# A Mamba and expert-choice kernel: stage 1's steps at other slots of the chunk, the expert stage written out without a loop

## What is computed

```python
x, z  = split(h @ in_proj_w.T)                  # 512 + 512 channels
u     = silu(causal_conv4(x) + conv_b)
dt, B, C = split(u @ x_proj_w.T, [16, 16, 16])
delta = softplus(dt @ dt_proj_w.T + dt_b)
state = exp(delta * A[n]) * state + delta * B[n] * u     # 16 states n, along the 2048 tokens
y     = sum_n C[n] * state + u * D
x1    = layernorm(x_in + (y * silu(z)) @ out_proj_w.T)
scores = softmax(x1 @ gate_w.T)                 # 8 experts
# each expert takes its 2048 highest tokens:
out   = gelu(layernorm(x1[idx]) * ln_w + ln_b @ fc1 + b1) @ fc2 + b2
x2    = x1; x2[idx] += out * score
return layernorm(x1 + x2)
```

## Time and profile before

| | |
|---|---|
| median of 3 runs | 4649.29 us (4644.24 to 4654.29) |
| the profiled execution | 4637.58 us, its span 4635.8 us |
| stage 1, first scan to last | 67.6 to 3470.5 us |
| stage 2 | 3530 to 3642 us |
| stage 3 | 3642 to about 4530 us, matmuls from 3706.7 to 4520 us |
| busy over the span | DVE 84%, PE 80%, POOL 76%, ACT 75% |
| granted TensorE clock, mean | 0.886 of full |

### The profile page before, as it was taken

The page is one execution under the profiler, slowest core; times in us unless marked ns, Lnnn a source line. Parts: engine busy times, 40 slices in busy tenths (PEclk is TensorE's granted clock), DMA queues, the critical chain, the costliest instruction groups (busy, mean ns, idle before and its releaser), DMA issues. The chain is left out here.

```text
span 4635.8 us, 58286 instructions
## 1 busy us (share of the span) xinstructions
PE 3700.9 (80%) x19154; PEld 2583.8 (56%) x19154; DVE 3909.9 (84%) x4971; ACT 3474.8 (75%) x5860; POOL 3515.7 (76%) x1714
## 2 busy tenths in 40 slices
PE   7788888888888888888888888888853199999990
PEld 3455555555555555555555555555542188888880
DVE  4899999999999999999999999999994677767645
ACT  5888888888888888888888888888860056555555
POOL 3888888898888888888888888888871156666643
PEclk9899899998988889989999998899965599999995
DMA  2666666665666666656665666666652123333328
GB/s 75 137 141 150 152 154 155 146 155 137 146 146 149 147 153 148 154 143 154 146 153 138 149 158 145 150 149 153 143 123 39 51 53 60 73 61 61 62 33 294
DMA packets 179913, 594.87 MB, mean 128 GB/s; under 512 B 33424, under 2 KB 99088, under 8 KB 128160
## 3 DMA queue, kind: packets, MB, share of 16 engines
q0 software_dynamic: 70368, 335.06, 36.8%
q1 hardware_dynamic: 104640, 239.32, 16.8%
q10 hardware_dynamic: 4608, 16.78, 0.9%
HBM read 221.47 MB, written 68.68 MB: 63 GB/s over the span
## 5 line engine op out<-in xcount | busy, mean ns | idle before, releaser
L433 POOL TENSOR_TENSOR dbu<-du,bb 128x2048 f32<-128x2048 f32 x512 | 2376.0, 4688 | 257.3 <-DVE h L793 229.4
L793 DVE TENSOR_TENSOR_SCAN h<-da,hlast,dbu 128x512 f32<-128x512 f32 x1536 | 1883.6, 1268 | 122.6 <-POOL dbu L433 79.0
L719 PE MATMUL ht<-ident,h 128*128 128x128 f32 x8192 | 1271.2, 305 | 503.1 <-DVE h L793 316.5
L485 ACT ACTIVATE da<-dl,negA 128x512 f32<-128x512 f32 x2048 | 1399.3, 693 | 278.3 <-DVE h L793 273.3
L719 PEld LDWEIGHTS ht<-ident,h 128*128 128x128 f32 x8192 | 1053.3, 157 | 965.9 <-DVE h L793 465.9
L504 ACT ACTIVATE pair<-ht,ct 128x512 f32<-128x512 f32 x768 | 517.9, 684 | 169.6 <-PE ht L719 138.9
L793 DVE TENSOR_TENSOR_SCAN h<-da,dbu 128x512 f32<-128x512 f32 x512 | 597.5, 1209 | 53.5 <-POOL dbu L433 27.3
L649 PE MATMUL spare<-xin,win 128*128 128x512 f32 x1024 | 513.6, 628 | 23.9 <-DVE conv L773 12.1
L655 PE MATMUL spare<-xh,conv 128*128 128x512 f32 x1024 | 474.8, 607 | 2.0 <-ACT dl L518 1.3
L801 DVE SCALAR_TENSOR_TENSOR pair<-ht,ct,pair 128x512 f32<-128x512 f32 x576 | 415.5, 731 | 21.9 <-PE ht L719 21.7
L1205 POOL DMA_INDIRECT sums<-ot,idx x128 | 237.3, 1854 | 172.6 <-DVE ot L1481 131.7
(11 more groups left out here) (163 smaller groups left out, 5860.2 us busy)
## 6 DMA issues: line engine op xcount, KB each, us to landing
acc<-pair POOLq DMA_DIRECT2D x192, 1024.0 KB, 7.1
bb<-b_rows SPq DMA_DIRECT2D x128, 1024.0 KB, 5.7
acc<-acc POOLq DMA_DIRECT2D x64, 1024.0 KB, 8.9
dl<-du POOLq DMA_DIRECT2D x62, 512.0 KB, 9.1
xin<-in_xt SPq DMA_DIRECT2D x32, 512.0 KB, 3.6
xres<-in_x SPq DMA_DIRECT2D x32, 512.0 KB, 5.7
x_scores<-xres SPq DMA_DIRECT2D x32, 512.0 KB, 3.0
sums<-xres SPq DMA_DIRECT2D x32, 512.0 KB, 4.1
```

The costliest lines, as they stand in the source:

```text
L433: pool.tensor_tensor(dbu[n % 2][:], du[q][:], bb[part % 2][:, m:m + 1, :].to_broadcast([P, DT, CH]), ALU.mult).then_inc(dbu_done, 1)
L485: act.activation(da[DA_SLOT[m]][:], dl[q][:, dt, :], ACT.Exp, scale=negA[:, dt, n:n + 1]).then_inc(exp_done, 1)
L719: last = te.transpose(ht[HT_SLOT[m]][:, dt * P:(dt + 1) * P], h[n % 2][:, dt, b * P:(b + 1) * P], ident[:])
L793: dve.tensor_tensor_scan(h[n % 2][:, dt, :], da[DA_SLOT[n * DT + dt]][:], dbu[n % 2][:, dt, :], start, ALU.mult, ALU.add).then_inc(scan_do ...
```

## The change

In stage 1 nothing is added or taken away; the tables are other ones. DVE keeps 28 multiply-adds and ACT 36 scales a chunk, in nine tiles with the same homes. On PE, C2 stands in slot 1 (was 2) ahead of Y0, C3 and the Ys one slot later than before or nearly, T0 in slot 4 (was 5), D2 in slot 7 (was 8), L0 in slot 10 (was 9), X2 in slot 14 (was 15). On DVE the Y read-outs move from (3,0), (3,3), (4,3), (5,3) to (4,1), (5,1) and twice (5,3), router 0 from (12,2) to (11,2), router 1 from (14,2) to (12,2), the statistics from (15,3) to (15,1). On POOL gate 0 to 2 move a slot later, the halo and gate 3 stand in slot 10, tile 2's add in slot 8 (was 7), tile 4's in slot 11 (was 12); the scores move to slot 14, and the first du multiply from slot 13 to slot 15, where all four now stand. In stage 3 the loop is gone, the weights are loaded first, with the second one of expert 0 in a buffer of its own (`hraw`), the two splits stand behind the eight one-hots and the index, rstd of the first group stands behind two gathers, the table of gelu is loaded ahead, and three one-hots of the second expert move from ahead of the first group into it. Cut to its core:

```diff
-STEPS = [(0, "C", 0), (1, "C", 1), (1, "Y", 0), (2, "C", 2), (2, "Y", 1), (2, "Y", 2), (3, "C", 3), (4, "Y", 3),
-         (5, "T", 0), (5, "XP", 0), (6, "T", 1), (7, "D", 0), (7, "CT", 0), (7, "D", 1), (8, "D", 2), (9, "D", 3),
-         (9, "O", 0), (9, "L", 0), (10, "O", 1), (11, "Z", 0), (12, "Z", 1), (12, "Z", 2), (13, "Z", 3),
-         (14, "X", 0), (14, "X", 1), (15, "X", 2), (15, "X", 3)]
+STEPS = [(0, "C", 0), (1, "C", 1), (1, "C", 2), (2, "Y", 0), (2, "C", 3), (3, "Y", 1), (3, "Y", 2), (4, "Y", 3),
+         (4, "T", 0), (5, "XP", 0), (6, "T", 1), (7, "D", 0), (7, "CT", 0), (7, "D", 1), (7, "D", 2), (9, "D", 3),
+         (9, "O", 0), (10, "L", 0), (10, "O", 1), (11, "Z", 0), (12, "Z", 1), (12, "Z", 2), (13, "Z", 3),
+         (14, "X", 0), (14, "X", 1), (14, "X", 2), (15, "X", 3)]
...
-DVE_AT = {(3, 0): [("Y", 0)], (3, 3): [("Y", 1)], (4, 3): [("Y", 2)], (5, 3): [("Y", 3)], (11, 1): [("O", 0)],
-          (12, 2): [("router", 0)], (13, 0): [("O", 1)], (14, 2): [("router", 1)], (15, 3): [("stats", 0)]}
+DVE_AT = {(4, 1): [("Y", 0)], (5, 1): [("Y", 1)], (5, 3): [("Y", 2), ("Y", 3)], (11, 1): [("O", 0)],
+          (11, 2): [("router", 0)], (12, 2): [("router", 1)], (13, 0): [("O", 1)], (15, 1): [("stats", 0)]}
...
-POOL_AT = {3: [("rstd", 0)], 5: [("gate", 0)], 6: [("gate", 1), ("gate", 2)], 9: [("gate", 3)], 11: [("halo", 0)],
-           12: [("delta_u", 0)], 13: [("delta_u", 1), ("delta_u", 2)],
-           15: [("delta_u", 3), ("scores", 0), ("delta_u", 4), ("delta_u", 5)]}
+POOL_AT = {3: [("rstd", 0)], 6: [("gate", 0)], 7: [("gate", 1), ("gate", 2)], 10: [("halo", 0), ("gate", 3)],
+           12: [("delta_u", 0)], 13: [("delta_u", 1)], 14: [("scores", 0)],
+           15: [("delta_u", 2), ("delta_u", 3), ("delta_u", 4), ("delta_u", 5)]}
...
-ADD_AT = {1: 6, 2: 7, 3: 10, 4: 12, 5: 13, 6: 15, 7: 16, 8: 18}
-BETWEEN = [0, 1, 2, 2, 2, 1, 0, 1, 1, 1, 0, 0, 1, 1, 1, 1]
+ADD_AT = {1: 6, 2: 8, 3: 10, 4: 11, 5: 13, 6: 15, 7: 16, 8: 18}
+BETWEEN = [0, 1, 0, 2, 1, 0, 0, 2, 1, 1, 1, 0, 1, 0, 2, 0]
...
-            def run(prologue, step, eng):
+            def run(prologue, step):
                 prologue()
-                for e in range(2):
+                for e in range(E):
                     for t in range(NG):
-                        step(e, t, e, True, True, 3)
-                with eng.Fori(1, E // 2 - 1) as j:
-                    for p in range(2):
-                        for t in range(NG):
-                            step(2 * j + p, t, p, True, True, 3)
...
                 def prologue():
                     gather(0, 0, 0)
                     gather(0, 1, 0)
+                    rstd_and_shift(0)
                     gather(0, 2, 0)
-                    rstd_and_shift(0)
...
-                act.wait_ge(small_in, 32)
+                act.preload_act_table_set("gelu_apprx_tanh_and_others")
...
                     for s in range(SL):
-                        if s in (3, 6):
-                            split_weights(0, 0, s // 3 - 1)
                         list_onehot(0, s)
                     list_index(0, 0)
+                    split_weights(0, 0, 0)
+                    split_weights(0, 0, 1)
                     row_stats(0, 0, 0)
```

More of the change, by code:

```diff
@@ L1085, in stage3 @@
         made, ident_ok, iotas, consts = S("made3"), S("ident3_ready"), S("iotas"), S("constants3")
-        small_in, w_in, b1_in = S("small_in"), S("weights_in"), [S(f"bias_in{i}") for i in range(2)]
+        small_in, w_in, b1_in = S("small_in"), [S(f"weights_in{i}") for i in range(2)], [S(f"bias_in{i}") for i in range(2)]
         rhs_ok, oh_ok, oh_used, idx_ok = S("rhs_steps"), S("onehot_ready"), S("onehot_used"), S("idx_ready")
@@ L1097, in stage3, with raw_weights @@
         yt_rest, h_rest = S("yt_rest_ready"), S("hidden_rest_ready")
+        def raw_weights(e, which):
+            return flat(hraw) if e == 0 and which == 1 else wraw[:]
         def rest_done(m, grp):
@@ L1155, in step @@
                         load_weights(e + 1, 1)
-                run(prologue, step, sp)
+                run(prologue, step)
             @block.gpsimd
@@ L1174, in gather @@
                         pool.wait_ge(idx_ok, e + 1)
-                    if not isinstance(e, int) or e > 0:
+                    if e > 0:
                         pool.wait_ge(ot_ok, grp - 3)
@@ L1199, in scatter @@
                     pool.wait_ge(ot_ok, e * NG + t + 1)
-                    if t == 0 and not (isinstance(e, int) and e == 0):
+                    if t == 0 and e > 0:
                         for k in range(NG):
@@ L1220, in step @@
                         scatter(e, t - 1, p)
-                    elif not (isinstance(e, int) and e == 0):
+                    elif e > 0:
                         scatter(e - 1, NG - 1, 1 - p)
@@ L1229, in step @@
                             gather(e + 1, t - 1, 1 - p)
-                run(prologue, step, pool)
+                run(prologue, step)
                 scatter(E - 1, NG - 1, 1)
@@ L1253, in turn_out @@
                         act.wait_ge(tp_ok, 2 * grp + k + 1)
-                        if not isinstance(grp, int) or grp > 0:
+                        if grp > 0:
                             act.wait_ge(yt_rest, 2 * (grp - 1) + k + 1)
@@ L1266, in step @@
                         act.wait_ge(f1_ok, grp * FM + m + 1)
-                        if m == 0 and not (isinstance(e, int) and grp == 0):
+                        if m == 0 and grp > 0:
                             act.wait_ge(f2_ok, grp * 4)
-                        if m >= HR or not (isinstance(e, int) and grp == 0):
+                        if m == 0 and grp == 0:
+                            act.wait_ge(w_rest, 2)
+                        if m >= HR or grp > 0:
                             s, v = rest_done((m - HR) % FM, grp if m >= HR else grp - 1)
@@ L1281, in prologue @@
                     normalise(0, 0)
+                    act.wait_ge(small_in, 32)
                     turn_out(0)
                     normalise(1, 1)
-                run(prologue, step, act)
+                run(prologue, step)
             @block.tensor
@@ L1321, in step @@
                     for m in range(FM):
-                        if m >= 2 or not (isinstance(e, int) and grp == 0):
+                        if m >= 2 or grp > 0:
                             te.wait_ge(gelu_ok, grp * FM + m - 1)
@@ L1330, in step @@
                     if following and t == 0:
-                        token_list(e + 1, range(0 if isinstance(e, int) and e == 0 else 2, 4))
+                        token_list(e + 1, range(0 if e == 0 else 2, 4))
                     if following and t == 1:
@@ L1341, in step @@
                     for b in range(4):
-                        if not (isinstance(e, int) and grp == 0) and b % 2 == 0:
+                        if grp > 0 and b % 2 == 0:
                             te.wait_ge(biased, 2 * (grp - 1) + b // 2 + 1)
@@ L1357, in step @@
                         last.then_inc(f2_ok, 1)
-                run(prologue, step, te)
+                run(prologue, step)
             @block.vector
@@ L1371, in list_rhs @@
                     hi = d["hi"][:, :, bass.ds(e, 1), :].rearrange("p s a g -> p s (a g)")
-                    if not (isinstance(e, int) and e == 0):
+                    if e > 0:
                         dve.wait_ge(oh_used, e * SL)
@@ L1383, in list_onehot @@
                 def list_onehot(e, s):
-                    if not (isinstance(e, int) and e == 0 and s < OH):
+                    if e > 0 or s >= OH:
                         dve.wait_ge(oh_used, e * SL + s - OH + 1)
@@ L1393, in list_index @@
                     dve.wait_ge(idxf_ok, e + 1)
-                    if not isinstance(e, int) or e > 1:
+                    if e > 1:
                         for k in range(NG):
@@ L1442, in prologue @@
                     rest_of_input(0)
-                    for s in range(4):
-                        list_onehot(1, s)
+                    list_onehot(1, 0)
                 def step(e, t, p, following, later, ahead):
@@ L1471, in step @@
                         rest_of_input(grp + 1)
-                    if not isinstance(e, int) or grp > 1:
+                    if grp > 1:
                         dve.wait_ge(added[(t - 2) % NG], 64 * (e + (1 if t >= 2 else 0)))
@@ L1482, in step @@
                     last.then_inc(ot_ok, 1)
-                run(prologue, step, dve)
+                run(prologue, step)
 def stage4(nc, d, n_tok):
```

52 lines of the change are left out of this document (31 added, 21 removed), and 28 rows, old and new, of tables (ACT_AT, MAC_AT, SCALE_AT).

## The result

The changed kernel takes 4490.43 us, median of 4 runs (4484.68 to 4495.45), beside 4646.76 (4635.27 to 4654.29) for the kernel before: a ratio of 0.967, 95% interval 0.9645 to 0.9688. That is 156 us less where the prediction said 38, and 55 us under the low end of its range. The profiled execution has a span of 4493.7 us (4635.8 before), 142.1 less.

The account below looks back on a forecast made before the run. DVE was taken to bound stage 1, though not alone, and TensorE stage 3. Terms of -14 us (stage 1) and -24 us (stage 3) gave -38: 4599.6 us profiled, 4611 us as the median forecast, range 4545 to 4668.

Parts of the forecast that it names:

- (a): Stage 1, end of a chunk: tile 6's add issued sooner, landing in 12.8 us; slot 1's scan 1.0 us sooner.
- (b): Stage 1, next chunk's start: slot 0's wait grows to about 0.8 us, slot 1's shrinks to about 1.6; gain stays 1.0.
- (c): Stage 1, slots 1 to 13: TensorE later at three places, DVE with less work; 0.55 us lost a chunk.
- (e): Stage 3 start: DVE no longer waits for `ln` and `b2`; 3.7 us won.
- (f): Stage 3 start: two splits leave the way to the index; 6.9 us won.
- (g): Stage 3 start: first group's rstd waits for eight gathers and not twelve; 5.0 us won.
- (h): Stage 3 start: splits beside first gathers cost 0.6 us, a slow gather leaves the way to rstd; net 1.2 us won.
- (i): Stage 3, first group: TensorE's wait for DVE's rest of hidden goes; 2.4 us won.
- (j): Stage 3, the loop's way back: its 2.85 us gap and the half clock behind it go; 4.6 us won.
- TensorE's clock: Slower rival, stage 1: TensorE stands still about 3 us at slot 5, half clock costs 2.0 us a chunk; 4674 us, chance 0.18.
- More is won: Rival, stage 1: slot 10's wait goes too, slot 1's add lands in 11 us; -2.5 us a chunk, 4547 us, chance 0.17.
- "issue" at slot 10: Sign in stage 1: DVE's scan wait at slot 10, 1.2 us a chunk before, should stay.

Follow-up runs that it names:

- POOL's slots and the scores back: Kernel before with the changed kernel's GpSimd slots, but the router's scores at their old place in slot 15: 4623.54 us, ratio 0.9943.
- the other three engines' slots: Kernel before with the changed kernel's slots of TensorE, ACT and DVE, GpSimd's as before: 4536.3 us, ratio 0.9758.
- the kernel with the load first: Changed kernel with the load of B's rows issued ahead of the wait for Z3 and the load of x: 4535.22 us, ratio 0.977.

## Why the prediction was wrong

**The step that failed is in (a): "lands 12.8 us later with the load still beside it ... the landing and not the slots sets it".** The prediction saw that the load ran beside the add, and wrote that this was so because both wait for `dbu` of slot 15. It did not ask what else stands in SyncE's queue ahead of that load: a wait for Z3, done at 94.2 us of the chunk, only 2.3 us before `dbu` 15 at 96.5, nor what the new tables do to Z3. With `dbu` 15 at 91.5 and Z3 at 93.1 the order turned, and the landing fell by 3.2 us. The size of this step is shown from both sides: 81 us when the load alone is held back in the kernel before, 48 us when it alone is put back beside the add in the changed one. The forecast's 1.0 us a chunk for slot 1 was 2.4.

**(a) and (b) as far as they went** had the right instants, with the waits of slots 0 and 1 within 0.35 us of their numbers; alone they gave 26 us by the ratio (16 to 37), where 31 were priced. The trace gives less, 0.4 us a chunk: over chunks 3 to 29 slot 0 had waited 0.18 us and not chunk 4's 0.5, so it lost 0.96 there.

**What turned the order.** `dbu` 15 was forecast 1.0 us earlier and came 5.0 earlier, counted from the chunk's first scan, since every wait that goes inside a chunk comes off all its later instants. But that moves Z3 as well and turns nothing: with the load held in the kernel before, `dbu` 15 comes 2.4 us sooner and Z3 is still done 2.2 us ahead of it, as before. Counted from slot 14's first scan, Z3 starts at 0.0 in the kernel before and with the load held, at 1.0 with POOL's slots and the scores back, and at 3.2 with the other three engines' slots and 3.1 in the changed kernel; `dbu` 15 ends there at 4.1, 4.1, 3.9, 4.3 and 3.4. So 3.2 of the 3.9 us by which the two changed places are Z3's later start, and 0.7 are `dbu` 15's. That the start is later because of `BETWEEN[13]` is read from the order of TensorE's rows above; no run changes that entry alone.

**(c) was forecast as a loss of 0.55 us a chunk and was a gain.** D2: the wait stays, as said (1.48 us at slot 10, 1.54 at (9,2)), and the reason given was right; D2 behind the turn takes it away in either kernel. Router 0: 0.38 at (11,2), against the 0.3 forecast. C2 ahead of slot 2's turn: 0.4 forecast, and the wait at (2,3), 0.27, went instead. Not in the sum at all were the waits of 0.4 to 0.7 us that the old tables had at slot 14 (0.72), at (15,3) (0.37) and at O0's read-out (0.48): the first was seen and counted as swallowed by the chain, which held only while the landing ended that chain. Over these the changed kernel is 1.3 us a chunk (41 us of stage 1) under the kernel before with the load held. Which table brings which of them wasn't tried.

**Stage 3.** Its sum came out, 25.6 us for 24, partly by luck: one term was too large and another too small by about as much. (e) 3.7 forecast, 3.9 measured. (f), (g), (h): 13.1 forecast, 6.8 measured. The first gather came 10.8 us nearer to the stage's start, as the sum of (e) and (f) says. From there on (g) and (h) had 6.2 us, and TensorE starts 26.9 us behind the first gather, where it was 26.8. Two things ate them. (h) was mis-sized: two gathers beside the splits took 2.27 and 2.73 us where others take 0.95, 3.1 us in all and not 0.6. (And the 2.71 us of the earlier trace rows, which it counts among the four gathers that leave the way, is the eighth of twelve and stays; the ninth, 2.02, leaves.) Missed altogether, rstd's small instructions now ran beside `list_rhs` of the second expert, 4.2 us. The Trainium skill, "SBUF — State Buffer", section "SBUF: two separate sides", says that VectorE and GpSimd share a pair of ports as an exclusive lock, which a VectorE instruction with two inputs in SBUF holds to its end against a GpSimd instruction that reads SBUF. The trace agrees: the first two small instructions of POOL above each end 0.1 us behind such an instruction of DVE (3568.11 and 3568.02; 3570.44 and 3570.34). Gathers show the same: the 2.71 us ended 0.82 us behind DVE's L1375 beside it (3691.66 and 3690.84), the 2.02 us 0.82 behind L1379, the 2.73 us 0.83 behind the second L1421 (3559.14 and 3558.31). (i) 2.4 forecast, 7.8 measured (36.5 to 28.7 us): the waits for ACT, 2.3 us, went too, and TensorE is busy 3 us less (31.7 to 28.7) for the same matmuls, at a mean clock of 0.91 and not 0.86. (j) 4.6 forecast, 4.9 measured. The 2.2 us that are left of the 25.6 are spread over the other groups.

**The rivals.** TensorE's clock: it does stand still where that rival said, for 1.9 us in front of T0 (mean; it waits for Y2's read-out), and half clock follows. The windows of 36 to 42 us of chunks 4 and 16 of the changed kernel both read:

```profile
516.30:522.30 6.00, 5.76 (x25) 3.97 (x26) 6.00 (x8) 5.94 (x8) 6.00 (x4) 0.72 0.83 172
1745.00:1751.00 6.00, 5.71 (x24) 3.93 (x25) 6.00 (x8) 5.94 (x8) 6.00 (x4) 0.72 0.87 171
```

A clock of 0.72 (3.4 of 6 us at 1.2 GHz) with DVE busy for all 6.00 us: DVE doesn't wait for it. "More is won" had the right mechanism for half (the add lands in 11 us or less) and 2.5 us a chunk; it was 3.7. Of the signs that the prediction named, "issue" at slot 10 went and a new wait for `ht` over 1 us a chunk came (1.54 at (9,2)), which it had named as a sign of being wrong; the clock stayed within the 0.02.

## What to carry to other kernels

When a transfer that sets the pace shares its moment with another, read what stands ahead of the *other* one in its queue: here a load that left 2 us later or not decided 48 to 81 us, and one line that holds it back was worth more than the whole forecast. To see whether a change turns the order of two instants, count both from the same instruction near them: what comes off the front of a period moves both, and what turned the order here was one step that now stands behind a turned block and not ahead of it. Put TensorE's side work behind a turned block that somebody waits for, and move a consumer only together with its producer: an instruction of 0.24 us placed ahead of its input cost 121 us.

## What the hardware showed that was not expected

A 1 MB accumulating DMA from POOL's queue and a 1 MB load from SyncE's don't split the time by how long they overlap. Over the 216 chunks of the table: with the load issued ahead of the add or up to 0.8 us behind it, the add takes 10.8 to 13.9 us and the load lands first, in all 109; with the load 1.3 us or more behind, the add takes 7.4 to 10.5 and lands first, in all 97, even where, at 2 us, most of the load still runs beside it. In between both happen: nine chunks of the three-engine kernel (1.0 to 1.2 us behind) had 8.3 to 9.4, one of the kernel with the load first (1.2) 13.3. The Trainium skill, "DMA: Bandwidth & Descriptors", section "Queues, rings and completion order", says that each DMA engine takes turns between queues packet by packet; by that alone a load 2 us later should lengthen the add nearly as much. The runs here show that it does not; they don't show why.
